# Value products in filter steps, first-layer rows between the sort's lookups, three tiles of mix products dealt over the last filter steps

## The reference

```python
xn = layernorm(x)
x = x + gnn(xn, src, dst, edge_attr_20, edge_weight, edge_attr_3, ...) + mix(xn)
x = x + ffn(layernorm(x))

def gnn(x, idx_i, idx_j, f_ij, rcut_ij, r_ij, ...):
    xs, xv = x[:, :C] @ W_in2f_s, einsum(x[:, C:], W_in2f_v)      # node table
    u = r_ij / norm(r_ij)
    W = (shifted_softplus(f_ij @ Wf1 + bf1) @ Wf2 + bf2) * rcut_ij  # filters, per edge
    agg = segment_sum(messages(xs[idx_j], xv[idx_j], u, W), idx_i)
    ...
def mix(x, Wq, Wk, Wv, Wo, bo):
    q, k, v = softmax(x @ Wq), softmax(x @ Wk), x @ Wv    # per head of 64
    return (q @ (k.T @ v)) @ Wo + bo
```

## Time and profile before

| | |
|---|---|
| median of 3 runs | 1273.39 us (1271.0, 1273.39, 1275.69) |
| profiled execution | 1271.56 us, span 1269.5 us, mean granted clock 0.97 |
| TensorE busy | 1190.8 us (94%) |
| VectorE busy | 1071.0 us (84%) |
| GpSimd busy | 870.8 us (69%) |
| ScalarE busy | 812.4 us (64%) |
| front, up to the first scatter | 0 to 79.51 us |
| filter loop on GpSimd | 79.51 to 494.7 us |
| sums on TensorE without long gaps | from 524.85 us |

### The profile page before, as it was taken

One profiled execution on the slowest core, in us unless ns is written; L12 is line 12 of the kernel. 1 busy time (PEld: TensorE's weight loads), 2 busy tenths in 40 slices (PEclk: granted clock), 3 DMA queues, 4 the chain that ended last, 5 costly groups with the idle time before them and its releaser, 6 DMA issues.

```text
span 1269.5 us, 16249 instructions
## 1 busy us (share of the span) xinstructions
PE 1190.8 (94%) x4108; PEld 700.0 (55%) x4108; DVE 1071.0 (84%) x1998; ACT 812.4 (64%) x1822; POOL 870.8 (69%) x795
## 2 busy tenths in 40 slices
PE   4999999989999999899999999999999999977995
PEld 3566666767766664344444444444444444766882
DVE  5958999899989995699999999999999997589325
ACT  3667777777767660576776767767767674775330
POOL 6357777777777775688888888888888881053650
PEclk8989999999999999899999999999999999987996
DMA  9248876887799966988888898988898881554557
GB/s 276 63 153 298 296 266 256 314 304 270 291 320 358 305 236 233 351 302 309 316 309 307 305 315 305 311 309 302 315 309 304 310 265 34 203 188 143 183 172 235
DMA packets 106608, 337.65 MB, mean 266 GB/s; under 512 B 16783, under 2 KB 17803, under 8 KB 100373
## 3 DMA queue, kind: packets, MB, share of 16 engines
q0 software_dynamic: 57264, 188.75, 41.5%
q1 hardware_dynamic: 49252, 147.88, 35.4%
HBM read 211.27 MB, written 125.30 MB: 265 GB/s over the span
## 4 chain that ended last, share of the span: by engine, by line
PE 76%; DVE 12%; DMA 4%; issue 3%; ACT 2%; POOL 1%; SPq 0%; DVEq 0%; POOLq 0%; ACTq 0%
PE PS L2306 22%; PE PS L2311 22%; PE PS L2242 11%; PE PS L2431 6%; DVE RR L1587 4%; PE PS L2109 3%; PE PS L2119 2%; PE PS L2087 2%; DMA X<-in_x 1%; DMA edge_records<-RR 1%; DVE h_low L1580 1%; PE PS L2240 1%; PE PS L2409 1%; POOL edge_records L953 1%; PE PS L2202 1%
## 5 line engine op out<-in xcount | busy, mean ns | idle before, releaser
L990 POOL DMA_INDIRECT RR<-node_table,RR x322 | 445.4, 1383 | 112.2 <-issue 64.0
L1250 ACT ACTIVATE RR<-RR 128x256 f32<-128x256 f32 x966 | 394.5, 494 | 194.1 <-PE PS L2311 155.6
L953 POOL DMA_INDIRECT edge_records<-RR x316 | 315.0, 997 | 107.3 <-issue 72.7
L2306 PE MATMUL PS<-RR 128*125 128x512 f32 x644 | 291.6, 595 | 3.8 <-DVE RR L1765 3.7
L2311 PE MATMUL PS<-RR 128*125 128x512 f32 x644 | 289.6, 592 | 0.0
L2306 PEld LDWEIGHTS PS<-RR 128*125 128x125 f32 x644 | 121.0, 189 | 162.1 <-issue 144.4
L2311 PEld LDWEIGHTS PS<-RR 128*125 128x125 f32 x644 | 120.9, 188 | 155.5 <-issue 155.5
L1587 DVE TENSOR_TENSOR RR<-PS,RR 128x512 f32<-128x512 f32 x237 | 161.0, 687 | 23.4 <-PE PS L2242 22.7
L2242 PE MATMUL PS<-wf_high,h_high 128*128 128x512 f32 x316 | 148.5, 470 | 8.7 <-DVE RR L1587 8.4
L1765 DVE TENSOR_TENSOR RR<-RR 128x1536 f32<-128x1536 f32 (+1 forms) x81 | 141.0, 1741 | 0.0
L2242 PE MATMUL PS<-wf_low,h_high 128*128 128x512 f32 x316 | 125.9, 398 | 0.0
(11 more groups left out here) (354 smaller groups left out, 1799.1 us busy)
## 6 DMA issues: line engine op xcount, KB each, us to landing
RR<-edge_records SPq DMA_DIRECT2D x48, 1040.0 KB, 6.6
expert_inputs<-RR SPq DMA_DIRECT2D x8, 2313.0 KB, 17.7
RR<-edge_records SPq DMA_DIRECT2D x27, 520.0 KB, 5.1
RR<-edge_records SPq DMA_DIRECT2D x15, 780.0 KB, 5.5
RR<-in_L_ffn_beta_w SPq DMA_DIRECT2D x8, 1024.0 KB
expert_w_raw<-in_L_ffn_expert_w SPq DMA_DIRECT2D x8, 1024.0 KB, 7.0
RR<-edge_records SPq DMA_DIRECT2D x31, 260.0 KB, 5.2
edge_records<-RR POOLq DMA_INDIRECT x322, 4.3
```

The lines of the kernel that those rows point to most:

```text
L953: g.indirect_dma_start(out=rec_dram, out_offset=place, in_=ST[:, j, :], in_offset=None).then_inc(scattered[c], 16)
L990: g.indirect_dma_start(out=GB[q % GBS][:, t, 1:5, :].rearrange("p k n -> p (k n)"), out_offset=None, in_=tab_dram, in_offset=bass.Indirect ...
L1250: last = a.activation(message_slot(q)[:, t, k:k + 5:4, :], GB[q % GBS][:, t, 0:k + 3:k + 2, :], ACT.Copy, scale=record_slot(q)[:, t, 4 * C ...
L2306: te.matmul(PS[0:NT, 2 * (r % PSS), :], OH[q % OHS][:, t, 0:NT], GB[q % GBS][:, t, 1:5, :].rearrange("p k n -> p (k n)"), start=(n == 0), ...
```

## The change

- **Front.** Of the ten value products five remain (FRONT = 5). The products and copies of table tiles 6 to 9 and the transposes of tiles 7 to 9 move between the transposes and first layers of filter steps 0 to 2, in another PSUM bank. VectorE's place lookups (`places_in_blocks`) are cut in three parts, with `hidden`, `low` and `stage_f_low` of the first steps between them. The reciprocal of the edge lengths moves ahead on VectorE, its root on ScalarE. SyncE loads the filter weights and the first features before Wq and Wk.
- **GpSimd.** Small fills move behind the places of the spare records; the six spare records are scattered one each after steps 1, 3, 5, 7, 9 and 11 of the loop.
- **Late values.** Wv is loaded a second time, over the sort's buffers, once the places are ready. Value products of tiles 5 to 9 go into the last step of attention tiles 0 to 4: products 0 and 1 behind column 0, product 2 behind column 1, product 3 behind column 3, into bank 6. ScalarE copies them at the start of the next step. The next query tile waits for that copy.
- **Blank rows** of the experts start at steps 16, 27, 37 and 50 instead of 3, 18, 34 and 50.
- **Mix.** Twelve products (tiles 0 to 2) go behind column 3 of steps 68 to 77, and behind columns 1 and 3 of step 78. VectorE adds tiles 0 and 1 in the steps after, tile 2 behind the loop; seven tiles of `mix` remain there. VectorE then adds all tiles before it turns to the first group of the sums.

```diff
+        EARLY_XT = 6
+        def xT_bank(t):
+            return t % 2 if t < EARLY_XT else 6
+        def table_bank(t):
+            return 2 if t < FRONT else 7
+        def value_bank(t):
+            return 3 + t % 2 if t < FRONT else 6
...
-        BLANK_STEP = [TILE_STEP] + [2 * CHUNK * k + 2 for k in range(1, BLANKS)]
+        SPARE_STEPS = range(1, 1 + 2 * (NCOL - LOOPED), 2)
+        BLANK_STEP = [SPARE_STEPS[-1] + 5, 27, 37, 50]
+        DEALT = 3
+        deal_at = [(WO_STEP + KD + u, 3) for u in range(DEALT * KD - 2)] + [(STEPS - 1, 1), (STEPS - 1, 3)]
+        dealt_in = [deal_at[n * KD + KD - 1][0] for n in range(DEALT)]
...
@@ SyncE @@
-            load_projection(WQ, Wq, wqkv_in[0])
-            load_projection(WK, Wk, wqkv_in[1])
-            load_features(0)
-            load_features(1)
             sp.wait_ge(edge_zero, 3)
...
+            load_features(0)
+            load_projection(WQ, Wq, wqkv_in[0])
+            load_projection(WK, Wk, wqkv_in[1])
+            load_features(1)
...
+            sp.wait_ge(edge_places, 2)
+            load_projection(WV_again, Wv, wqkv_in[2])
@@ GpSimd @@
-            for n in range(NCOL - LOOPED):
-                spare_record(LOOPED + n)
             pool.wait_ge(edge_places, 2)
             for m in range(STEPS):
                 scatter(m // RING, m % RING)
+                if m in SPARE_STEPS:
+                    spare_record(LOOPED + SPARE_STEPS.index(m))
@@ ScalarE, in filters @@
+                if r == 0 and 1 <= t <= NB - FRONT:
+                    values(FRONT + t - 1)
                 if exists(i, c + 1):
                     high(i, c + 1)
                 first_column(i, c)
...
-            bias_rows()
-            table_rows(NB - 1)
             radial(0, 0)
             stage_f(2)
-            values(NB - 2)
+            table_rows(6)
+            evac_xT(7)
             log_part(0, 0)
             radial(0, 1)
+            stage_f(3)
+            table_rows(7)
+            evac_xT(8)
+            log_part(0, 1)
             high(0, 0)
-            stage_f(3)
-            values(NB - 1)
-            log_part(0, 1)
             radial(0, 2)
             stage_f(4)
+            table_rows(8)
+            evac_xT(9)
+            bias_rows()
+            table_rows(9)
+            log_part(0, 2)
             radial(0, 3)
-            log_part(0, 2)
@@ VectorE @@
+            places_in_blocks(range(0, 3))
+            hidden(0, 0)
             stage_f_low(0, 2)
-            hidden(0, 0)
+            places_in_blocks(range(3, 6))
+            low(0, 0)
+            hidden(0, 1)
+            stage_f_low(0, 3)
+            places_in_blocks(range(6, NB))
+            edge_rows()
+            stage_f_low(0, 4)
             dve.wait_ge(b2_ready, 1)
-            low(0, 0)
-            stage_f_low(0, 3)
-            hidden(0, 1)
-            stage_f_low(0, 4)
             dve.wait_ge(dirs_ready, 1)
-            dve.wait_ge(v_psum, NB)
-            for s in range(2):
-                dve.wait_ge(tab_out[s], 32 * (NB // 2))
+            dve.wait_ge(v_psum, FRONT)
...
+                if m - 1 in dealt_in[:-1]:
+                    add_mix(dealt_in.index(m - 1))
...
+            add_mix(DEALT - 1)
             mixing_weights()
             zero_sums(0)
-            for n in range(NB):
...
+            for n in range(DEALT, NB):
+                done = 2 * (n - DEALT)
+                for part in range(done + 1, min(done + 3, ZERO_PARTS)):
+                    zero_sums(part)
                 add_mix(n)
@@ TensorE @@
+            def late_value(t, k):
+                if t == FRONT and k == 0:
+                    pe.wait_ge(wqkv_in[2], 64)
+                if k == 0:
+                    pe.wait_ge(qT_ready, t - FRONT + 1)
+                last = te.matmul(PS[0:NT, value_bank(t), :], XTQ[:, t, k, :], WV_again[:, k, :], start=(k == 0),
+                                 stop=(k == KD - 1))
+                if k == KD - 1:
+                    last.then_inc(v_psum, 1)
...
+            def dealt_mix(u):
+                n, k = divmod(u, KD)
+                if u == 0:
+                    pe.wait_ge(mo_ready, KD)
+                elif k == 0:
+                    pe.wait_ge(mix_added, n)
+                mix_product(n, k)
...
+            pe.wait_ge(w_rounded, 1)
             transposes(0, 0)
-            value_product(NB - 2)
+            table_product(6)
+            transpose_x(7)
             pe.wait_ge(wf2_l, 1)
+            pe.wait_ge(xT_ready, EARLY_XT)
             layer1(0, 0)
             transposes(0, 1)
-            value_product(NB - 1)
-            pe.wait_ge(tab_ready, NB)
+            table_product(7)
+            transpose_x(8)
+            pe.wait_ge(tab_ready, FRONT)
             layer1(0, 1)
             transposes(0, 2)
+            table_product(8)
+            transpose_x(9)
+            pe.wait_ge(w_rounded, 5)
+            pe.wait_ge(v_ready, FRONT - 1)
+            te.matmul(PS[:, 4, :], ones2[:, :], b2hl[:, :], start=True, stop=True).then_inc(b2_psum, 1)
+            table_product(9)
             layer1(0, 2)
             transposes(0, 3)
...
-                elif 0 <= t < NB and r == PER - 1 and j == 2:
-                    context(t)
+                elif 0 <= t < NB and r == PER - 1:
+                    if j == 2:
+                        context(t)
+                    elif t < NB - FRONT:
+                        for k in ((0, 1), (2,), (), (3,))[j]:
+                            late_value(FRONT + t, k)
...
+                elif (m, j) in deal_at:
+                    dealt_mix(deal_at.index((m, j)))
...
-            for n in range(NB):
+            for n in range(DEALT, NB):
                 mix(n)
```

More of the change, by code:

```diff
@@ L338, in gps_layer @@
         assert c1_early <= c2.at - 2 * P and c2.at <= acc_at
-        in_hidden = 4 * 512 // RC1
-        mask_at = [hidden_at + b * RC1 if b < in_hidden else kn_at + (b - in_hidden) * RC1 for b in range(NB)]
-        assert c1_early <= hidden_at and (NB - in_hidden) * RC1 <= 3 * D
+        FRONT = 5
+        in_values = (NB - FRONT) * D // RC1
+        mask_at = [vn_at + FRONT * D + b * RC1 if b < in_values else kn_at + (b - in_values) * RC1 for b in range(NB)]
+        assert c1_early <= hidden_at and (NB - in_values) * RC1 <= 2 * D
         block_mask = [R1[:, w:w + RC1] for w in mask_at]
@@ new lines, in _ @@
+            table_rows(2)
+            evac_xT(3)
+            moments_of((6, 7))
+            values(2)
+            table_rows(3)
+            evac_xT(4)
+            moments_of((8, 9))
+            later_std(slice(6, NB), NB - 1)
+            a.preload_act_table_set("natural_log_exp_and_others")
+            rounded_weights()
+            stage_f(0)
+            stage_f(1)
+            values(3)
+            table_rows(4)
+            evac_xT(5)
+            values(4)
+            table_rows(5)
@@ L1168, in radial @@
+            evac_xT(6)
+            act.wait_ge(w_ordered, 2)
+            a.activation(b2hl[0:2, :], b2f, ACT.Copy).then_inc(w_rounded, 1)
             def radial(i, c):
@@ L1559, in stage @@
                     dve.wait_ge(scattered[c], i * (16 * STEP))
+                elif c == 2:
+                    dve.wait_ge(tab_psum, NB)
+                elif c == 3:
+                    for s in range(2):
+                        dve.wait_ge(tab_out[s], 32 * (NB // 2))
                 v.tensor_copy(ST[:, c * STEP:(c + 1) * STEP, 4 * C:REC], meta[:, cols, :]).then_inc(staged, 1)
@@ L2089, in value_product, with block_counts @@
                 last.then_inc(v_psum, 1)
[L2091 to L2102 removed]
+            def block_counts():
+                pe.wait_ge(counts_ready, NB)
+                te.matmul(PS[:, 5, 0:NB], ltri[:, :], cnt, start=True, stop=True)
+                te.matmul(PS[:, 5, NB:2 * NB], ones[:, 0:P], cnt, start=True, stop=True).then_inc(counts_psum, 1)
+            def late_value(t, k):
[7 more added lines that the diff above has]
+                    last.then_inc(v_psum, 1)
+            table_product(0)
+            value_product(0)
+            table_product(1)
+            value_product(1)
+            transpose_x(2)
+            table_product(2)
+            transpose_x(3)
+            value_product(2)
+            table_product(3)
+            transpose_x(4)
+            value_product(3)
+            table_product(4)
+            transpose_x(5)
+            value_product(4)
+            table_product(5)
+            transpose_x(6)
+            block_counts()
             def query(t, k):
```

196 lines of the change are left out of this document (85 added, 111 removed).

## The result

The changed kernel took **1277.42 us** (median of 20 runs, 1274.27 to 1279.85) against 1272.88 us for the kernel before, run beside it (20 runs): a ratio of **1.0031, interval 1.0022 to 1.0039**. It is slower by 0.3%, some 4.5 us. By the 0.5% bound of the prediction it is "no change".

The account below looks back on a forecast made before the run. GpSimd's scatters were taken as the bound, with TensorE starving them at step 33. -3.6 there and -1.3 at the sums gave -4.9 us: 1266.7 against the profiled execution, 1268.5 us on the median's scale, range 1261 to 1277.

Parts of the forecast that it names:

- 0.5% bound: What a measurement can tell from no change, 6.4 us: under 1267.0 us is faster, over 1279.8 slower.
- Front, -11.5: Before the filter steps: five value products leave, so the first scatter comes at 68.0 us instead of 79.51; bounds -13, -8.5.
- Spare records, +7.6 with 2.4 in gaps: Six scatters moved into the loop's first steps cost GpSimd 7.6 us, about 2.4 of it in gaps it had.
- Late values, 2.16 each: Last step of five attention tiles: 3.44 us each on TensorE, 1.28 into slack; say +11 us by step 33.
- ScalarE's rival: ScalarE's copy of late values holds up each next step's columns: 4.8 us a tile, 1281.5 us, slower; chance 0.08.
- Step 33: GpSimd at 251.3, lag 3.6: TensorE at 247.7 us plus the least lag feeding GpSimd, 3.6, puts GpSimd at 251.3 instead of 254.90: -3.6 us.
- GpSimd bounds again and T moves by the same 3.6: After step 33 TensorE needs 29.8 us a tile, GpSimd 31.5, so the last scatter ends at 491.1 us.
- T: End of GpSimd's last scatter, 494.7 us in the kernel before, forecast 491.1; the end of the kernel follows it.
- the 3.1 us of lag: GpSimd's distance behind TensorE at step 33 that may be drained: 6.7 less the least 3.6 us.
- Dealt mix, free: Twelve mix products of 0.86 us in steps 68 to 78 fit narrowly: 5.1 us a step against GpSimd's 5.24.
- -1.3 at the sums: With less mixing behind the loop, the fifth gather no longer waits and TensorE's 1.31 us gap goes; bounds 0, -2.
- The clock rival: A longer gap before the sums drops TensorE's clock: costs 1.7 to 3.4 us, nothing regained, 1272.4 us; chance 0.13.

## Why the prediction was wrong, step by step

- **Front, -11.5.** Right within its bounds: 10.5 us, first scatter 68.97 for 68.0. The granted clock from 27 to 64 us was 0.85, where I had read 0.93 for the kernel before.
- **Spare records, +7.6 with 2.4 in gaps.** Right in size: up to step 9 four of them cost 5.0 us, of which 2.5 fell in gaps. Two things weren't in it: the waits for landings at steps 17 to 19, and that GpSimd's pause moved from step 28 to step 40.
- **Late values, 2.16 each.** Right in sum, for two reasons of which I had one. Steps 9 to 33 took (247.49 - 113.68) / 4 = 33.45 a tile instead of 31.08, 2.4 more; about 2.5 us of the four tiles are the stalls at steps 18 and 19, from landings. The rest is some 1.75 a tile instead of 2.16: the slack took more than I credited. ScalarE's rival fell, no step was near 4.8 longer.
- **Step 33: GpSimd at 251.3, lag 3.6.** Right to 0.2 us, but for GpSimd this is luck. The forecast had TensorE starve it there, with several waits in steps 20 to 33. Behind its first scatter GpSimd didn't wait once up to step 33: it came to 251.07 by its own rate, for which I had 248.6. The 2.5 us between are 1.0 of the later first scatter and 2.7 of longer scatters, less 1.0 of pause that the kernel before had at step 28. TensorE's 247.49 was forecast well, so the lag had shrunk to 3.6 all the same.
- **"GpSimd bounds again and T moves by the same 3.6": this is the step that failed.** I compared averages, 29.8 us a tile for TensorE, from steps 45 to 51, and 31.5 for GpSimd, from the whole loop, and let them hold from step 33 on. Between lie steps 38 and 39, 8.24 and 6.9 us long on TensorE, against GpSimd's 5.24. Five us of lag drain there (8.6 to 3.7), and I had just spent the reserve. The -3.6 was booked as a gain and the 3.1 us of lag that paid for the rest of the late values as free. Measured, steps 33 to 41 cost 5.0 us more: that turned -3.8 at step 33 into +1.2. Of these, 2.4 us are columns that came too late for the short lag, 1.7 of them at the run tables; the runs show that cause from both sides, by taking it away in the changed kernel and by making it in the kernel before. Another 2.4 us are GpSimd's pause, at step 40 now and exposed by the short lag; this is read from the traces and was not tested by a run of its own.
- **The remaining 1.8 us up to T** lie almost wholly in longer scatters: counting each one's time over 0.96 us, steps 41 to 79 hold 6.9 us of it after and 5.2 before. It differs between executions as well (steps 41 to 64 of the changed kernel took 120.9 and 122.6 us). Steps 9 to 33 lost 2.4 us in the same way.
- **Dealt mix, free.** Right. Steps 68 to 77 take (481.60 - 435.54) / 10 = 4.61 us, less than the 5.1 I gave, since a part of each 0.86 fell into gaps.
- **-1.3 at the sums.** Wrong. GpSimd's 5.66 us wait is gone (waits of 2.40 and 1.78 stand there), and so is TensorE's 1.31, but the fifth group of sums starts at 552.27, T + 54.6, against 548.76, T + 54.1, before. TensorE and VectorE at the beginning of the sums, as changed:

```profile
524.62 3.75 PE L2408 MATMUL PS<-RR 128*125 128x512 f32 x4 [13.68 <-DVE RR L1822]
528.16 2.64 PE L2413 MATMUL PS<-RR 128*125 128x512 f32 x4
531.01 3.67 PE L2408 MATMUL PS<-RR 128*125 128x512 f32 x8 [0.20 <-DVE RR L1822]
...
538.46 3.67 PE L2408 MATMUL PS<-RR 128*125 128x512 f32 x8 [0.35 <-DVE RR L1822]
```
```profile
521.59 1.23 DVE L1793 TENSOR_TENSOR RR<-RR 128x1024 f32<-128x1024 f32 x1 [6.05 <-DMA RR<-node_table,RR]
```

  VectorE waits for the second group of gathered rows until T + 23.9; before, it had them at 515.13, T + 20.4. Mixing ends long before (its last product ends at T + 13.2), TensorE then idles 13.68 us, and a gap of 1.31 further on has nothing to give. Why that gather lands later behind the same T I didn't test.
- **The clock rival** was wrong in size. The first group's eight instructions took 3.75 + 2.64 us where the kernel before needed 1.95 + 1.88 for the same eight, while its next eight took 5.37; now those take 3.67. One group with the lower clock in it, not two: the granted clock is 0.50 from 524.6 to 528.2 us, 0.73 to 531, and 1.00 from there to 540. The Trainium skill, "TensorE: Matmul & The Clock Gate", section "Why this matters for your kernels", warns of such a gap because the clock falls back in it; this trace agrees. The price was 2.6 us once, and it replaced one of 1.7 (5.37 less 3.67) rather than adding to it, so 0.9 was lost where the rival had 1.7 to 3.4.

## What to carry to other kernels

Where one engine runs behind another through a ring, read the distance between them at every step, not at the ends: it is a reserve which short blocks of other work draw on, and it is useful only as far as the ring also holds the time that its entries take to land. An edit that fills the slower-looking engine's slack spends that reserve, so look for the next long step behind it (here a block of 3.9 us on a third engine, six steps on) and move that block to where the reserve is full. An average rate over a stretch says which engine bounds only if the reserve holds every long step in it. And where a profile names what ended a wait, look up when the thing that was really needed was ready: here the longest wait of all was put down to a column which it didn't need.

## What the runs showed of the hardware

**Pause.** GpSimd stood for 3.13 us between two of its instructions at the same two places of its program, in all 17 traces. It cost 2.4 us where GpSimd had just caught up with VectorE and nearly nothing where it was 5.8 us behind. A trace with a wait longer than its cause deserves this look.

**Landing.** A scatter of 128 records landed after 2.7 us where no other large transfer ran, and after 8.6 us beside the blank rows. Such a stretch makes a ring of staging buffers shorter.

**Longer scatters.** A scatter takes GpSimd 0.96 us, or up to 1.5. Many of the long ones lie beside certain operations of VectorE. Two stretches of GpSimd's and VectorE's common timeline in the changed kernel:

```profile
229.71 0.96 POOL L972 DMA_INDIRECT edge_records<-RR  x1 [0.30 <-issue]
229.79 0.67 DVE L1543 TENSOR_REDUCE small<-RR 125x8 f32<-125x512 f32 x1
...
230.74 0.69 DVE L1545 TENSOR_TENSOR RR<-RR,small 125x512 f32<-125x512 f32 x1
230.97 1.30 POOL L972 DMA_INDIRECT edge_records<-RR  x1 [0.30 <-issue]
...
239.99 0.69 DVE L1545 TENSOR_TENSOR RR<-RR,small 125x512 f32<-125x512 f32 x1
240.16 1.35 POOL L972 DMA_INDIRECT edge_records<-RR  x1 [0.30 <-issue]
```

Beside the reduction, with one input in SBUF, the scatter keeps 0.96; begun within the L1545, with two, it takes 1.30 and 1.35. Over 22 scatters that overlap an L1545 the mean excess is 0.20 us, over 104 that overlap the low part of h (L1633) 0.08. The Trainium skill, "SBUF — State Buffer", section "Who interferes with whom", says that an instruction of VectorE with two SBUF inputs contends with one of GpSimd that reads SBUF; these rows agree, and the price here is 0.3 to 0.4 us for the two shown. It was seen, not tested: no run changed the overlap on purpose. How much of the 4.7 us between the two kernels' 316 scatters comes from it isn't shown.
